# An FFN and convolution kernel: identity loads, the order of the first transfers, chunk 0's normalisation and the 1/sqrt of chunks 2 and 3 are moved in its opening

## The reference

```python
x = L0_attn_u                                  # (4, 512, 512) f32, 2048 tokens of 512
xn = _layernorm(x, axis=-1)                    # (x - mean) / sqrt(var + 1e-5)
# S4 branch: a kernel K of 512 taps from Lambda, p, q, Ct, B, then a causal convolution over the last axis
y = irfft(rfft(xn, n=1024) * rfft(K, n=1024))[..., :512] + D[0] * xn
# FFN branch, weights stored as NF4 codes (16 values) and one absmax for 64 weights
Wg, Wu = dequant_nf4(gate_q, ...), dequant_nf4(up_q, ...)      # (1792, 512)
Wd = dequant_nf4(down_q, ...)                                  # (512, 1792)
ffn = (silu(xn @ Wg.T) * (xn @ Wu.T)) @ Wd.T
return x + y + ffn
```

## Time and profile before

| | us |
|---|---|
| median of 3 runs (lowest to highest) | 508.47 (508.27 to 508.72) |
| the profiled execution's own time | 508.43 |
| its span in the trace | 506.7 |
| PE busy | 475.2 (94%) |
| DVE busy | 290.6 (57%) |
| ACT busy | 211.2 (42%) |
| POOL busy | 23.5 (5%) |

### The profile page before, as it was taken

How to read it: one execution, slowest core, us unless ns; L and a number is a source line. 1 busy time by engine, 2 the same in 40 slices (tenths; PEclk the granted TensorE clock), 3 DMA queues, 4 the chain that set the end, 5 groups by cost and what they waited for, 6 DMA issues and landing times.

```text
span 506.7 us, 6088 instructions
## 1 busy us (share of the span) xinstructions
PE 475.2 (94%) x2283; PEld 224.7 (44%) x2283; DVE 290.6 (57%) x537; ACT 211.2 (42%) x371; POOL 23.5 (5%) x80
## 2 busy tenths in 40 slices
PE   0278999999999999999999999999999999999997
PEld 0243444444444444444444464456544444444443
DVE  3888676665656567685667848765677623000013
ACT  3475846445544555445454434668654000000000
POOL 0005334000000000000000000000000000000000
PEclk9998999999999999999999999999999999999999
DMA  7834582111111111112111111224432612200013
GB/s 217 276 87 108 104 223 69 63 41 59 48 61 43 41 63 62 43 41 59 50 60 41 43 41 43 83 74 121 139 88 59 210 40 76 91 0 1 0 39 128
DMA packets 32829, 39.77 MB, mean 78 GB/s; under 512 B 16224, under 2 KB 16544, under 8 KB 32800
## 3 DMA queue, kind: packets, MB, share of 16 engines
q1 hardware_dynamic: 32512, 39.32, 26.6%
q10 hardware_dynamic: 288, 0.07, 0.1%
HBM read 32.03 MB, written 4.19 MB: 71 GB/s over the span
## 4 chain that ended last, share of the span: by engine, by line
PE 92%; DVE 3%; DMA 2%; ACT 1%; SPq 1%; issue 1%
PE bank L1019 57%; PE bank L1121 29%; PE bank L1111 5%; DMA qs<-in_q_up 2%; PE bank L1084 1%; DMA xT<-h 1%; ACT h L484 1%; DVE h L678 0%; SPq L278 0%; ACT h L496 0%; DVE h L722 0%; DVE xT L720 0%; ACT w L454 0%; PE bank L1044 0%; ACT xT L496 0%
## 5 line engine op out<-in xcount | busy, mean ns | idle before, releaser
L1019 PE MATMUL bank<-xT,w 128*128 128x512 f16 x1344 | 292.3, 380 | 5.9 <-DMA xT<-h 3.8
L1019 PEld LDWEIGHTS bank<-xT,w 128*128 128x128 f16 x1344 | 131.6, 98 | 165.4 <-DMA xT<-h 3.9
L1121 PE MATMUL bank<-wd,h 128*128 128x512 f16 x672 | 145.2, 379 | 0.0
L447 ACT ACTIVATE knee<-qs 128x512 f32<-128x512 int32 x164 | 97.9, 619 | 11.8 <-DMA qs<-in_q_gate 11.7
L1121 PEld LDWEIGHTS bank<-wd,h 128*128 128x128 f16 (+1 forms) x672 | 65.7, 98 | 79.0
L624 DVE SCALAR_TENSOR_TENSOR bank<-bank,sc,sil 128x512 f32<-128x512 f32 x56 | 42.5, 758 | 70.1 <-PE bank L1019 62.3
L475 ACT ACTIVATE h<-bank 128x512 f16<-128x512 f32 x56 | 33.3, 595 | 68.2 <-DVE bank L624 68.2
L1005 DVE SCALAR_TENSOR_TENSOR xT<-bank,sc,xT 128x512 f32<-128x512 f32 x16 | 11.4, 748 | 84.1 <-PE bank L1121 84.1
L469 ACT ACTIVATE sil<-bank,sc 128x512 f32<-128x512 f32 x56 | 37.9, 677 | 19.0 <-PE bank L1019 19.0
L629 DVE TENSOR_TENSOR h<-bank,h 128x512 bf16<-128x512 f32 x56 | 38.6, 690 | 9.9 <-ACT h L475 8.6
L590 DVE SCALAR_TENSOR_TENSOR acc_r<-knee 128x512 f32<-128x512 f32 x41 | 28.1, 686 | 20.4 <-ACT knee L447 20.4
(11 more groups left out here) (95 smaller groups left out, 132.0 us busy)
## 6 DMA issues: line engine op xcount, KB each, us to landing
h<-in_x SPq DMA_DIRECT2D x8, 512.0 KB, 11.2
w<-in_x SPq DMA_DIRECT2D x16, 256.0 KB, 3.6
out<-xT SPq DMA_DIRECT2D x16, 256.0 KB, 2.0
qs<-in_q_gate SPq DMA_DIRECT2D x14, 256.0 KB, 2.6
qs<-in_q_up SPq DMA_DIRECT2D x14, 256.0 KB, 2.7
am<-in_am_gate SPq DMA_DIRECT2D x28, 128.0 KB, 2.9
am<-in_am_up SPq DMA_DIRECT2D x28, 128.0 KB, 2.9
qs<-in_q_down SPq DMA_DIRECT2D x14, 256.0 KB, 2.6
```

The source lines that it names most:

```text
L447: nc.scalar.activation(knee_of(u, k), qs[:, u % 2, :], KNEE, scale=scale, bias=bias, alpha=below).then_inc(knee_done, 1)
L1019: mm = nc.tensor.matmul(out_b[:], w1[:, k % 2, unit, wl, f, :], xT[:, TPC * c:TPC * c + TPC, xl, f, :], start=(i == 0), stop=(i == 3 * NC ...
L1121: mm = nc.tensor.matmul(bank[(t + 4) % 8][:], part, wd[:, mt, wl, :], start=(mt == 0 and n == 0), stop=(mt == NM - 1 and n == 2))
```

## The change

The identity loads go from ACT's queue to SP's, behind the first codes and the first tokens. The codes of the first up unit are loaded ahead of tiles 2 to 7, and the absmax rows and the third unit's codes behind them. All four tiles of chunk 0 are normalised on DVE. The 1/sqrt of chunks 2 and 3 goes from POOL to DVE, in two more groups of 13 `rstd` instructions, set one by one among weight steps. The last four `scales` are moved behind the first weight unit. The order of ACT's and DVE's lists is written anew up to window 3.

```diff
@@ -208,7 +208,6 @@
         rs_step = sem("rs_step")
-        rs_pool = sem("rs_pool")
         xn0_done = sem("xn0_done")
@@ -241,7 +240,6 @@
         RSTD = 13
-        RSTD_POOL = 17
         EXP_STEPS = 7 + EXP_TERMS
@@ -280,14 +278,16 @@
             sp.dma_start(xs[:, 0:2, :], x_v[:, 0:2, :]).then_inc(x_ld[0], 16)
+            sp.dma_start(id_row, root_rows[0:1, 0:P].to_broadcast([P, P])).then_inc(id_ld, 16)
+            sp.dma_start(id_col, cos_cols).then_inc(id_ld, 16)
             sp.dma_start(amf, am_flat).then_inc(amf_ld, 16)
+            load_codes(1, q_up[0])
             sp.dma_start(xs[:, 2:4, :], x_v[:, 2:4, :]).then_inc(x_ld[1], 16)
-            load_codes(1, q_up[0])
-            load_absmax(0, am_gate[0])
             sp.dma_start(xs[:, 4:6, :], x_v[:, 4:6, :]).then_inc(x_ld[2], 16)
             sp.dma_start(xs[:, 6:8, :], x_v[:, 6:8, :]).then_inc(x_ld[3], 16)
+            load_absmax(0, am_gate[0])
+            load_codes(2, q_gate[1])
             load_absmax(1, am_up[0])
-            load_codes(2, q_gate[1])
             for i in range(4, 8):
@@ -337,31 +337,6 @@
-            rs_n = [0]
-            def rs_next(op, *args, wait=True):
-                if wait:
-                    pool.wait_ge(rs_pool, rs_n[0])
-                op(*args).then_inc(rs_pool, 1)
-                rs_n[0] += 1
-            for c in range(2, NCH):
-                a, b = TPC * c, TPC * c + TPC
-                hv, y, t, nm = (rs[:, i, a:b] for i in range(4))
-                pool.wait_ge(mv_done, b)
-                rs_next(pool.tensor_scalar, y, mv[:, a:b, 1], EPS, 1.0, ALU.add, ALU.mult, wait=False)
-                rs_next(pool.tensor_scalar, hv, mv[:, a:b, 1], EPS, -0.5, ALU.add, ALU.mult, wait=False)
-                rs_next(pool.tensor_scalar, nm, mv[:, a:b, 0], -1.0, 0.0, ALU.mult, ALU.add, wait=False)
-                rs_next(pool.tensor_scalar, y.bitcast(I32), y.bitcast(I32), -0.5, float(RSQRT_MAGIC),
-                        ALU.mult, ALU.add)
-                for last in (False, False, True):
-                    rs_next(pool.tensor_tensor, t, y, y, ALU.mult)
-                    rs_next(pool.tensor_tensor, t, t, hv, ALU.mult)
-                    rs_next(pool.tensor_scalar, t, t, 1.5, XS if last else 1.0, ALU.add, ALU.mult)
-                    rs_next(pool.tensor_tensor, rs[:, 4, a:b] if last else y, y, t, ALU.mult)
-                rs_next(pool.tensor_tensor, rs[:, 5, a:b], nm, rs[:, 4, a:b], ALU.mult)
             pool.wait_ge(step_ld, 16)
@@ -430,8 +405,6 @@
         def _(act):
-            act.dma_start(id_row, root_rows[0:1, 0:P].to_broadcast([P, P])).then_inc(id_ld, 16)
-            act.dma_start(id_col, cos_cols).then_inc(id_ld, 16)
             act.wait_ge(one_done, 1)
@@ -476,10 +449,8 @@
             def norm(t):
-                if t < 8:
-                    act.wait_ge(rs_step, RSTD)
-                else:
-                    act.wait_ge(rs_pool, RSTD_POOL * (t // TPC - 1))
+                act.wait_ge(rs_step, RSTD if t < 8 else RSTD * (t // TPC))
+                if t >= 8:
                     act.wait_ge(xlo_done, t - 7)
@@ -489,7 +460,7 @@
                 else:
-                    act.wait_ge(xn_done, t - 1)
+                    act.wait_ge(xn_done, t - TPC + 1)
                     src, dst = xnb[:, t % 8, :], xst[:, t % 8, HI, :]
@@ -498,17 +469,13 @@
             items(13, 15)
-            norm(2)
-            x_hi(0)
-            norm(3)
-            x_hi(1)
             weight_hi(0)
-            x_hi(2)
-            x_hi(3)
+            for t in range(4):
+                x_hi(t)
             norm(4)
-            weight_hi(1)
             norm(5)
             x_hi(4)
+            weight_hi(1)
             norm(6)
@@ -518,31 +485,33 @@
             nc.scalar.activation(yv[:, 0:2], bank[7][:, 0:2], ACT.Copy).then_inc(b_cp, 1)
-            items(20, 25)
+            items(20, 22)
+            items(23, 25)
             silu(1)
             norm(8)
-            h_hi(0)
+            weight_hi(3)
             norm(9)
...
             x_hi(10)
+            h_hi(0)
             x_hi(11)
             h_hi(1)
+            silu(2)
             items(25, 27)
-            items(28, 30)
-            silu(2)
             norm(12)
...
             x_hi(13)
-            silu(3)
             norm(15)
...
             x_hi(15)
+            silu(3)
+            items(28, 30)
             h_hi(3)
@@ -596,7 +565,7 @@
                     if u == 0:
-                        dve.wait_ge(sc_done, SCALES)
+                        dve.wait_ge(sc_done, WEIGHT_SCALES)
                     dve.wait_ge(am_ld[u % 2], 32 * (u // 2 + 1))
@@ -645,7 +614,7 @@
-            SPREAD, SCALES = 7, 13
+            SPREAD, WEIGHT_SCALES, SCALES = 7, 9, 13
@@ -682,14 +651,14 @@
-            def rstd(i):
-                a, b = 0, 2 * TPC
+            def rstd(g, i):
+                a, b = ((0, 8), (8, 12), (12, 16))[g]
                 var, hv, y, p, r = mv[:, a:b, 1], rs[:, 0, a:b], rs[:, 1, a:b], rs[:, 2, a:b], rs[:, 3, a:b]
...
                 else:
-                    dve.wait_ge(rs_step, i)
+                    dve.wait_ge(rs_step, RSTD * g + i)
                 newton = (i - 3) % 3
@@ -725,85 +694,112 @@
             step(0, 1)
+            stats(1)
             dve.wait_ge(id_ld, 32)
...
             scales(0)
-            stats(1)
+            step(1, 0)
             scales(1)
+            step(1, 1)
+            scales(2)
             stats(2)
-            scales(2)
-            step(1, 0)
             scales(3)
...
             scales(4)
-            step(1, 1)
+            stats(4)
             scales(5)
             scales(6)
-            stats(4)
+            stats(5)
+            stats(6)
             scales(7)
-            stats(5)
+            stats(7)
             scales(8)
-            stats(6)
-            scales(9)
-            stats(7)
-            scales(10)
             moments(0, 8)
-            scales(11)
-            rstd(0)
-            scales(12)
-            rstd(1)
-            rstd(2)
+            rstd(0, 0)
+            rstd(0, 1)
+            rstd(0, 2)
             step(0, 2)
-            rstd(3)
-            rstd(4)
+            rstd(0, 3)
+            rstd(0, 4)
             step(0, 3)
-            rstd(5)
-            rstd(6)
+            rstd(0, 5)
+            rstd(0, 6)
             step(0, 4)
             for i in range(7, RSTD):
-                rstd(i)
-            norm(0)
-            norm(1)
+                rstd(0, i)
+            for t in range(TPC):
+                norm(t)
+            weight_lo(0)
             step(1, 2)
+            for t in range(TPC):
+                x_lo(t)
             step(1, 3)
-            weight_lo(0)
-            x_lo(0)
-            x_lo(1)
             step(1, 4)
-            x_lo(2)
-            x_lo(3)
+            x_lo(4)
+            for i in range(WEIGHT_SCALES, SCALES):
+                scales(i)
+            weight_lo(1)
+            for t in range(5, 8):
+                x_lo(t)
             items(12, 14)
-            weight_lo(1)
-            for t in range(4, 8):
-                x_lo(t)
-            items(15, 18)
             stats(8)
+            items(15, 16)
             stats(9)
-            items(18, 20)
+            items(16, 17)
             stats(10)
+            items(17, 18)
             stats(11)
             moments(8, 12)
-            items(20, 24)
+            items(18, 19)
+            rstd(1, 0)
+            rstd(1, 1)
+            items(19, 20)
+            rstd(1, 2)
+            rstd(1, 3)
+            items(20, 21)
+            rstd(1, 4)
+            rstd(1, 5)
+            items(21, 22)
+            for i in range(6, 9):
+                rstd(1, i)
+            items(22, 23)
+            for i in range(9, RSTD):
+                rstd(1, i)
+            items(23, 24)
             h_mul(0)
-            items(24, 27)
+            weight_lo(3)
+            x_lo(8)
+            items(24, 25)
+            x_lo(9)
+            items(25, 26)
+            x_lo(10)
+            h_lo(0)
+            x_lo(11)
+            h_mul(1)
             for t in range(12, 16):
...
             moments(12, 16)
-            h_lo(0)
-            for t in range(8, 10):
-                x_lo(t)
-            h_mul(1)
-            for t in range(10, 12):
-                x_lo(t)
+            for i in range(4):
+                rstd(2, i)
+            items(27, 28)
+            rstd(2, 4)
+            rstd(2, 5)
             h_lo(1)
-            items(27, 30)
+            rstd(2, 6)
+            rstd(2, 7)
+            items(28, 29)
+            rstd(2, 8)
+            rstd(2, 9)
+            items(29, 30)
+            for i in range(10, RSTD):
+                rstd(2, i)
+            h_mul(2)
             x_lo(12)
-            h_mul(2)
+            h_lo(2)
             x_lo(13)
-            h_lo(2)
             h_mul(3)
-            for t in range(14, 16):
-                x_lo(t)
+            x_lo(14)
+            x_lo(15)
             h_lo(3)
```

(5 more changed lines are left out.)

## The result

Measured in turns with the kernel before, the changed kernel takes 510.56 us (median of 6, 509.94 to 511.18) against 508.37 (507.98 to 508.72): ratio 1.0042, 95% interval 1.0030 to 1.0055. The forecast was 511.5, range 508.9 to 513.2.

A forecast was written before the change was run, and what follows sets the result against it. PE, holding 92% of the chain of waits, was taken to bound the kernel. 508.43 us plus 1.7 for chunk 3's later landing plus 1.4 for the clock made 511.5 us, range 508.9 to 513.2.

The forecast's parts named there:

- a later landing of chunk 3: Before n = 6: chunk 3's last turn lands at 70.4 instead of 68.7, adding 1.7 us.
- the clock: Behind the stop before n = 6: PE at half clock loses 1.39 us, bounds 0 and 2.0.
- Part 1: Opening transfers: up codes land at about 10.0, first tokens at 8.03 as before, norm(0) at 21.8, 0.84 earlier.
- Parts 2 to 4: Chunks 0 to 2: windows start 1.9 us earlier, n = 1 2.8 earlier, n = 4 could start 4.0 earlier.
- (a): Rival: the same lateness of chunk 3 without the clock loss, 510.1 us; chance 0.15.
- (d): Rival: up codes land at 11.7 as before, all of DVE 1.7 us later, 513.2 us; chance 0.07.
- Part 5: Chunk 3: norm(12) at 58.35 instead of 56.31, silu(3) delays x_lo(14), last turn lands 1.7 us later at 70.4.
- (b): Rival: DVE about 1.7 us faster, chunk 3 lands at 68.7, gap and clock loss remain, 508.4 to 509.8; chance 0.10.
- (c): Rival: the early start is kept, n = 4 starts at 54.5, norm(12) by 52.8, 504.6 us; chance 0.08.

The follow-up runs named there:

- a_id_act: The changed kernel with the two identity loads put back on ACT's queue; 510.66 us.
- b_id_sp: The kernel before with only the two identity loads moved to SP's queue; 507.12 us, ratio 0.9975.
- a_hmul_late: The changed kernel with h_mul(3) on DVE moved from ahead of x_lo(14) to behind x_lo(15); 508.81 us, ratio 1.0007.
- a_early: The changed kernel with stats(12) to stats(15) ahead of x_lo(8) to x_lo(11), unit 4's steps and h_lo(1) behind the 1/sqrt, h_mul(3) behind x_lo(15); 505.05 us.
- a_pool_c3: The changed kernel with the 1/sqrt of chunk 3 back on GpSimd, its statistics left in place; 511.99 us, ratio 1.0069.
- a_fill6: The changed kernel with 20 idle matmuls on PE in the stop ahead of n = 6; 510.54 us.
- a_early_h: a_early with h_mul(3) put back ahead of x_lo(14); 505.67 us, ratio 0.9955.

## Why the prediction was right, and what in it was luck

The time and the place came out: a stop of over 5 us before n = 6 (5.06, forecast 5.6), half clock behind it, no stop before n = 4, and `h_mul` waiting for `silu(3)` just ahead of `x_lo(14)`. The sum did not come out term by term. It was +1.7 for a later landing of chunk 3 and +1.4 for the clock; measured were -0.1 and +2.65 in the profile, +2.2 together in the medians. Chunk 3 landed at 68.6, as before, and not at 70.4. The forecast had given a sign of its own being wrong, turn(15) issued before 65.5, and that is what happened:

```profile
L276 SPq DMA_TRANSPOSE xT<-h x12: 1231/1328/1348, 28.4 to 65.3; - x12
```

So the step "landing 70.4 instead of 68.7: 1.7 us later" failed, and that 511.5 stands 0.9 us from the measured 510.56 is luck: a first term too large by 1.8 us and a second too small by 1.3.

**Part 1, the landing of the first transfers, was mis-sized by 2 us.** I put the first tokens at 8.03 as before, the up codes at 10.0 and norm(0) at 21.8. Measured: up codes at 8.09, norm(0) at 19.73. The up codes' landing accounts for 1.9 of the 2.07 us. I took 255 KB/us between two landings of before as the rate of the stream and let the up codes queue behind the late tokens; with the loads still on ACT they landed at 8.60, not at 10. The identity loads' move had "nothing", and 0.26 us at most. At the first codes it is worth 2 us (a_id_act, b_id_sp) and in the kernel before 1.4 us of time, so it was mis-sized as well; but in the changed kernel it can't be told from the spread of the up codes' landing, 8.09 to 9.23. The Trainium skill ("DMA: Bandwidth & Descriptors", issuing engines are not separate DMA queues) says that the DMAs of all queues interleave on the same engines. That the sharing costs no more than the bytes of the small loads was my own inference from it; the runs show 1.9 to 2.1 us for 66 KB.

**Parts 2 to 4 were right in their steps** and 1.7 to 2.3 us late in their clock times for that reason: windows from 28.6 (26.28), n = 1 at 37.45 (35.79), norm(8) at 43.7 (41.93). Small slips: three times 1.37 us behind 30.05 is 34.16, not 34.25, and the chances of the forecast, (a) and (d) alone make 0.82 for slower, where 0.81 stands. One small miss: the second unit's weights were to be ready before PE; it waits 0.20 us for them, and up to 1.07 in other runs of this opening.

**Part 5 was right in length.** From norm(8) to norm(12) I had 14.65 us, and it took 14.59. From norm(12) to the landing of the last turn I had 12.05, it took 12.1. a_hmul_late confirmed the 1.7 us of `silu(3)` (1.69), a_early and a_pool_c3 that `norm(12)` goes by what stands ahead of it on DVE: statistics, weight steps and `h_lo(1)`.

**The clock was mis-sized the other way:** 1.39 us by the one stop of before, 2.65 behind a longer stop. What the change costs in time hangs on this term, and a_fill6 leaves it partly open, since its median is no lower. My upper bound was 2.0. In the other profiles the loss is anything from 0 (a_early_h, 3.23 us without work) to 2.95 (a_hmul_late, 3.52 us). One row of one stop is no price; it should have been a range of 0 to 3.

Of the rivals, (a) falls: the clock did fall. Its ground was a misreading too: the granted clock of 1.00 in the first microseconds doesn't show a full clock after idleness, for `warm_up`'s matmuls ran at half rate there (0.229 us each against 0.117), so the rule of the Trainium skill ("TensorE: Matmul & The Clock Gate", Part 1) that the prediction had the first microseconds disagree with, half rate as the default state, agrees with these durations. (b), chunk 3 landing 1.7 us sooner at 68.7, came out in effect (68.6), for another reason, the early opening; it is the clock's other 1.3 us that kept the time above (b)'s 508.4 to 509.8. (c) needed norm(12) by 52.8; a_early nearly gives it that (53.8), and takes 505.05 us where (c) had 504.6. (d) fell with the early codes.

## What to carry to other kernels

Before an order is rewritten, find the one transfer that has no slack (here the last turn of chunk 3) and follow the path to it through every queue; everything that is won ahead of it turns into one long stop, and behind the stop PE's clock can be lower as well (0 to 2.95 us here). An instruction with a wait of its own (`h_mul(3)`) must not stand ahead of work that feeds that transfer, statistics whose inputs landed long ago can fill the idle moments of the engine, and weight steps that nobody waits for yet can stand behind the work that feeds it.

## What the runs showed of the hardware that was not expected

Two small loads on a second DMA queue (64 KB of row broadcasts and 2 KB in 16-byte pieces), issued beside SP's first loads, delayed the first 256 KB on SP's queue from 2.8 us after issue to 4.7 and 4.8, and the first tokens from 3.6 and 3.7 us to 6.2 and 6.8 (both pairs of kernels). From 2.4 to 4.2 us all DMA together moved 381 and 390 GB/s with the loads on SP (changed kernel, b_id_sp), 152 and 175 with them on ACT (a_id_act, the kernel before): the whole stream was slower, by much more than the bytes of the two loads. And the granted clock after a stop of 3.2 us is not a constant of the kernel: the same opening gave 0.50 in most profiles and 1.00 in that of a_early_h. A granted clock of 1.00 in the first microseconds of a profile is to be checked against the duration of the matmuls there; in the kernel before those of `warm_up` took twice as long as the same matmuls in a_fill6.
